# Attention scores of a 16-head transformer stack: from 96-row stacks of four heads to 32x128 row tiles, one strip of partitions per head

## The reference

```python
scores = einsum('bqhd,bkhd->bhqk', q, k) * scale      # per head, contraction over 8
scores = where(mask == 0, -1e9, scores)               # in A2, AS, A3 only
attn   = softmax(scores, axis=-1)
out    = einsum('bhqk,bkhd->bqhd', attn, v)
x      = x + out @ wo + bo
```

## Time and profile before

| | |
|---|---|
| runs | 2376.47, 2366.19, 2374.96 us; median 2374.96 |
| span of the profiled execution, first to last instruction | 2364.8 us |
| what lies around it, if it is one of the three runs (the profile does not say which) | 1.4 to 11.7 us |
| TensorE matmuls | 2118.7 us busy, 14264 instructions |
| TensorE weight loads | 1391.1 us, beside the matmuls |
| VectorE | 1247.3 us |
| ScalarE | 1289.5 us |
| GpSimd | 499.4 us |
| mean granted TensorE clock | 0.932 of 2.4 GHz |
| HBM traffic | 117.53 MB, 49 GB/s over the span |

### The profile page before, as it was taken

How to read it: one execution, slowest core, us unless ns; L and a number is a source line. 1 busy time by engine, 2 the same in 40 slices (tenths; PEclk the granted TensorE clock), 3 DMA queues, 4 the chain that set the end, 5 groups by cost and what they waited for, 6 DMA issues and landing times. The chain is left out here.

```text
span 2364.8 us, 46942 instructions
## 1 busy us (share of the span) xinstructions
PE 2118.7 (90%) x14264; PEld 1391.1 (59%) x14264; DVE 1247.3 (53%) x3806; ACT 1289.5 (55%) x2226; POOL 499.4 (21%) x1107
## 2 busy tenths in 40 slices
PE   2999975699997999979999978887997999989998
PEld 1555543355555889844554545555885555548887
DVE  5667646566662222256666544444564667642343
ACT  0777752377774444346666644444331787864443
POOL 4221210111211222121111111222232222212221
PEclk9999987699998999979999978788997899999999
DMA  3322310622310000052213011110003423300000
GB/s 81 90 80 54 94 29 0 169 71 64 89 40 10 1 0 0 1 143 67 69 45 85 28 41 42 54 54 10 0 0 101 119 72 76 89 1 1 4 4 10
DMA packets 101314, 117.53 MB, mean 50 GB/s; under 512 B 12710, under 2 KB 68412, under 8 KB 101180
## 3 DMA queue, kind: packets, MB, share of 16 engines
q1 hardware_dynamic: 101180, 115.94, 18.5%
HBM read 70.82 MB, written 45.09 MB: 49 GB/s over the span
## 5 line engine op out<-in xcount | busy, mean ns | idle before, releaser
L929 PE MATMUL ps_s<-kst,qz 96*128 96x512 f32 (+2 forms) x1280 | 601.2, 485 | 60.6 <-DMA qz<-q_parts 40.4
L758 ACT ACTIVATE prob<-ps_t 128x512 f32<-128x512 f32 (+1 forms) x896 | 492.3, 581 | 265.7 <-PE ps_t L941 109.9
L941 PE MATMUL ps_t<-qz,kst 128*128 128x512 f32 (+1 forms) x1152 | 464.5, 407 | 0.5 <-ACT prob L758 0.2
L1313 DVE CUSTOM_DVE_ANT_0 junk<-ps_s,mask_q 128x512 bf16<-128x512 f32 x512 | 342.1, 688 | 167.1 <-PE ps_s L929 160.4
L1304 DVE TENSOR_REDUCE mx<-ps_s 128x1 f32<-128x512 f32 x512 | 334.5, 684 | 138.5 <-PE ps_s L929 137.3
L929 PEld LDWEIGHTS ps_s<-kst,qz 96*128 96x128 f32 x1280 | 256.4, 205 | 237.1 <-DVE mx L1313 59.9
L961 PE MATMUL ps_av<-prob,vaug 128*32 128x256 f32 (+1 forms) x4608 | 363.5, 390 | 3.4 <-ACT avs L794 3.1
L1160 PEld LDWEIGHTS ps_s<-w_ffn,prob 128*128 128x128 f32 x2688 | 315.4, 192 | 8.7
L1160 PE MATMUL ps_s<-w_ffn,prob 128*128 128x128 f32 x2688 | 319.2, 276 | 0.0
L798 ACT ACTIVATE qz<-ps_m 32x1024 fp32r<-32x1024 bf16 x160 | 162.7, 1017 | 152.6 <-PE ps_m L971 149.0
L941 PEld LDWEIGHTS ps_t<-qz,kst 128*128 128x128 f32 x1152 | 225.0, 197 | 33.7 <-issue 9.8
(11 more groups left out here) (200 smaller groups left out, 2403.3 us busy)
## 6 DMA issues: line engine op xcount, KB each, us to landing
kst<-k_parts SPq DMA_DIRECT2D x32, 768.0 KB, 6.1
k_parts<-k_hi SPq DMA_DIRECT2D x64, 256.0 KB, 2.9
qz<-q_parts SPq DMA_DIRECT2D x160, 96.0 KB
q_parts<-q_hi SPq DMA_DIRECT2D x80, 128.0 KB, 2.4
ctxT<-in_ctxT SPq DMA_DIRECT2D x32, 256.0 KB, 4.7
k_parts<-k_lo SPq DMA_DIRECT2D x32, 256.0 KB, 2.9
q_parts<-q_lo SPq DMA_DIRECT2D x40, 128.0 KB, 2.4
w_ffn<-in_F_w SPq DMA_DIRECT2D x18, 256.0 KB, 3.9
```

What stands on the lines that cost most here:

```text
L758: nc.scalar.activation(dst, src, ACT.Exp, bias=bias).then_inc(sig["exp_done"], 1)
L929: pe.matmul(ps_s[TURN[i]][:, 0:nk], qz[p][0:96, g, j, q * 128:(q + 1) * 128], kst[p][0:96, g, 0:nk], start=True, stop=True).then_inc(sig[" ...
L941: mm = pe.matmul(dst, kst[p][:, g, kt * 128:(kt + 1) * 128], qz[p][:, g, 2 * half:2 * half + 2, q0:], start=True, stop=mask in (None, "keys"))
L1313: dve.tensor_tensor_reduce(junk[:, TURN[i], 0:nk], src, m, 1.0, -3.0e38, ALU.add, ALU.max, mx[:, buf, i:i + 1])\
```

## The change

The head gets a strip of 32 partitions (24 rows of parts, 8 of the maxima or of ones), and each score matmul contracts over its strip of 32 rows only, as a 32x128 tile of the array. `HEAD_S` and `HEAD_T` say which head's strip a beat uses: the transposed scores of beat n use strip (n+2) mod 4, the scores for the maxima strip n mod 4.

- `qz` with its zeros goes; `qst` holds 32 rows a head, `kst` likewise. The maxima are added in `maxima_T`: one fp32r identity matmul brings `qst` into PSUM and two bf16 matmuls add the three pieces, and ScalarE copies 256 columns into `qmx`, from which `scores_T` reads.
- `scores_T` takes one head and two key tiles: two matmuls of 256 columns on one strip with two weight loads where there was one of 512 columns for two heads. The mask of A2 and of AS is still one identity matmul of 128 rows behind them. In A3 the key mask becomes a matmul of one row (a row of the strip) behind each score matmul: one behind `scores`, two in `scores_T`.
- With the mask in PSUM, VectorE's maxima in A3 are plain reductions, and ScalarE's exponentials have no bias. All maxima are taken negated, so GpSimd's multiplication by -1 goes.
- `k_hi` and `q_hi` are written by GpSimd from `kf` and `qf`, except in AS.
- SyncE loads each group by itself: two DMAs for each of four groups, where there were one for the keys and four for the queries. The semaphores are per group.
- In a beat the transposed scores are issued first, the scores for the maxima second. In AS the four units of transposed scores stand at k = 0 and k = 3 (before: k = 0 and k = 2).
- Setup: `qz` and `kst` are not filled any more; `q_lo`, `k_lo`, `ident_r`, `ones_b` are, and four DMAs write the fill rows to the scratch.

The core of the diff:

```diff
+HEAD_S = [0, 1, 2, 3, 0, 1, 2, 3]
+HEAD_T = [2, 3, 0, 1, 2, 3, 0, 1]
...
+            def load_strips(ph, bt):
+                p, nk = bt.parity, ATT[ph]["nk"]
+                sp.wait_ge(k_saved[p], saved(ph, bt))
+                sp.wait_ge(q_saved[p], saved(ph, bt))
+                for g in range(NG):
+                    sp.dma_start(kst[p][:, g, 0:nk].bitcast(F32), scratch["k"][p][128 * g:128 * (g + 1), 0:nk]).then_inc(stacked[p][g], 16)
+                    sp.dma_start(qst[p][:, g, :].bitcast(F32), scratch["q"][p][128 * g:128 * (g + 1), :]).then_inc(stacked[p][g], 16)
...
             def split_k(ph, bt):
                 pool.wait_ge(sig["k_read"], cnt.at("k_read", ph, bt))
+                if ph != "AS":
+                    apart(pool)
+                    pool.tensor_copy(k_hi[:, 0:nk], kf[:, 0:nk]).then_inc(sig["k_hi_done"], 1)
+                pool.wait_ge(sig["k_hi_done"], cnt.at("k_hi_done", ph, bt))
...
             def maxima_T(ph, bt, g):          # ScalarE
-                nc.scalar.activation(qz[bt.parity][96:128, g, :, :], ps_mb[96:128, :].rearrange("p (j s) -> p j s", j=HG),
-                                     ACT.Copy).then_inc(sig["mt_read"], 1)
+                nc.scalar.activation(qmx[:, g % 2, :], ps_m[:, 0:S], ACT.Copy).then_inc(sig["mt_read"], 1)
...
             def scores(ph, bt, g, i):         # TensorE
-                p, nk, j, q = bt.parity, ATT[ph]["nk"], i // 2, i % 2
+                p, nk, j, q = bt.parity, ATT[ph]["nk"], HEAD_S[i], i // HG
+                strip = slice(STRIP * j, STRIP * (j + 1))
-                pe.matmul(ps_s[TURN[i]][:, 0:nk], qz[p][0:96, g, j, q * 128:(q + 1) * 128], kst[p][0:96, g, 0:nk],
-                          start=True, stop=True).then_inc(sig["s_ready"], 1)
+                mm = pe.matmul(dst, qst[p][strip, g, q * 128:(q + 1) * 128], kst[p][strip, g, 0:nk],
+                               start=True, stop=ATT[ph]["mask"] != "keys")
+                if ATT[ph]["mask"] == "keys":
+                    mm = pe.matmul(dst, ones_b[STRIP * j:STRIP * j + 1, 0:128], mrow[STRIP * j:STRIP * j + 1, p, :], start=False, stop=True)
...
             def scores_T(ph, bt, g, n):
-                mm = pe.matmul(dst, kst[p][:, g, kt * 128:(kt + 1) * 128], qz[p][:, g, 2 * half:2 * half + 2, q0:],
-                               start=True, stop=mask in (None, "keys"))
+                for c in range(2):
+                    kt = 2 * kp + c
+                    dst = bank[:, S * c:S * (c + 1) - seen(ph, kt)]
+                    mm = pe.matmul(dst, kst[p][strip, g, kt * 128:(kt + 1) * 128], qmx[strip, g % 2, seen(ph, kt):],
+                                   start=c == 0 or mask in (None, "keys"), stop=mask is None)
+                    if mask == "keys":
+                        mm = pe.matmul(dst, mrow[STRIP * j:STRIP * j + 1, p, kt * 128:(kt + 1) * 128], ones_b[STRIP * j:STRIP * j + 1, :],
+                                       start=False, stop=True)
                 if mask == "full":
+                    mm = pe.matmul(bank[:, :].rearrange("p (c s) -> p c s", c=2), ident_b[:, :], mask_T[:, 2 * kp:2 * kp + 2, :],
+                                   start=False, stop=True)
...
             def maxima_T(ph, bt, g):          # TensorE
-                for j in range(HG):
-                    for q in range(QT):
-                        mm = pe.transpose(ps_mb[96:128, S * j + 128 * q:S * j + 128 * (q + 1)],
-                                          mpart[:, g % 2, q, 32 * j:32 * j + 32], ident_b[:, :])
+                pe.matmul(ps_m[:, 0:S], ident_r[:, :], qst[bt.parity][:, g, :], start=True, stop=False)
+                for q in range(QT):
+                    mm = pe.matmul(ps_m[:, 128 * q:128 * (q + 1)], mpart[:, g % 2, q, :], ident_b[:, :], start=False, stop=q == QT - 1)
...
                             for half in range(2):
+                                if unit_at(ph, k, half) is not None:
+                                    scores_T(ph, bt, g, unit_at(ph, k, half))
                                 if ahead[0]:
                                     scores(*ahead, 2 * k + half)
-                                if kt is not None:
-                                    scores_T(ph, bt, g, kt, half)
```

More of the change, by code:

```diff
@@ L361, in seen, with pairs, unit, unit_at @@
             return 128 * kt if ph == "AS" else 0
-        def turn_of(ph, g, kt, half):
-            return (2 * (ATT[ph]["nk"] // 128 * g + kt) + half) % 8
+        def pairs(ph):
+            return ATT[ph]["nk"] // (2 * 128)
+        def unit(ph, g, n):
+            return HG * pairs(ph) * g + n
+        def unit_at(ph, k, half):
+            if pairs(ph) == 2:
+                return 2 * k + half
+            return {0: 0, 3: 2}[k] + half if k in (0, 3) else None
+        def chance(ph, g, n):
+            return prob[:, g % 2, HEAD_T[n], :], 2 * (n // HG)
         def slots(ph):
@@ L426, in _ @@
             load_attention("A0", loaded_first)
+            sp.wait_ge(setup_pool, 3)
+            for p in range(2):
+                for n, fill, w in (("q", q_lo, S), ("k", k_lo, SK)):
+                    rest = scratch[n][p].rearrange("(h b c) w -> b h c w", h=H, b=STRIP // DH)[PARTS]
+                    sp.dma_start(rest, fill[:, 0:w].bitcast(F32)).then_inc(strips_filled, 16)
             def load_rest():
@@ L748, in _, with exponentials @@
         def _(act):
-            def exponentials(ph, bt, g, kt, half):
-                p, nkt, q0 = bt.parity, ATT[ph]["nk"] // 128, seen(ph, kt)
-                bias = mcol[:, p, kt:kt + 1] if ATT[ph]["mask"] == "keys" else 0.0
-                wait(act, "st_ready", cnt.at("st_ready", ph, bt, 2 * (nkt * g + kt) + half))
-                if half == 0:
-                    wait(act, "av_ready", cnt.at("av_ready", ph, bt, nkt * g + kt) - 2 * nkt)
-                dst = prob[:, g % 2, kt, 2 * S * half:2 * S * (half + 1)].rearrange("p (j s) -> p j s", j=2)[:, :, q0:]
-                src = ps_t[TURN[turn_of(ph, g, kt, half)]][:, 0:2 * (S - q0)].rearrange("p (j s) -> p j s", j=2)
-                nc.scalar.activation(dst, src, ACT.Exp, bias=bias).then_inc(sig["exp_done"], 1)
+            def exponentials(ph, bt, g, n):
+                nkt = ATT[ph]["nk"] // 128
+                wait(act, "st_ready", cnt.at("st_ready", ph, bt, unit(ph, g, n)))
+                if n % HG == 0:
+                    wait(act, "av_ready", cnt.at("av_ready", ph, bt, nkt * g + 2 * (n // HG) + 1) - 2 * nkt)
+                row, kt = chance(ph, g, n)
+                w = 384 if ph == "AS" else 2 * S
+                nc.scalar.activation(row[:, S * kt:S * kt + w], ps_t[TURN[unit(ph, g, n) % 8]][:, 0:w], ACT.Exp).then_inc(sig["exp_done"], 1)
             def misc(what, ph, bt):
@@ L957, in values @@
                         wait(pe, "v_read", cnt.at("v_read", ph, bt))
-                wait(pe, "exp_done", cnt.at("exp_done", ph, bt, 2 * (nkt * g + kt) + 1))
+                wait(pe, "exp_done", cnt.at("exp_done", ph, bt, unit(ph, g, HG * (kt // 2) + HG - 1)))
                 buf = g % 2
```

171 lines of the change are left out of this document (81 added, 90 removed).

## The result

The changed kernel takes 2636.03 us (median of 4 runs, 2604.12 to 2693.75), the kernel before 2372.03 (median of 4). The ratio, 1.099 with a 95% interval of 1.093 to 1.105, is that of the two faster runs of the changed kernel, 2604.12 and 2617.57 us at mean granted clocks of 0.782 and 0.777, where the slowest had 0.748. Slower, as forecast, but by 264 us by the medians instead of 107, and outside the range of 2335 to 2580. The profiled run is that of 2654.48 us.

The account below looks back on a forecast made before the run. TensorE's order of work was taken to bound four phases. A1 -33, A0 -27, A2 +65, A3 +78, AS +27 and phase starts -3 gave +107 on 2364.8; with 10.2 to the median, 2482 us, range 2335 to 2580.

Parts of the forecast that it names:

- the clock being what it is: Condition on AS's term of +27 us (bounds 0 and +60): the granted clock was taken as unchanged.
- rival (d): TensorE's work looks thinner and the clock falls, mean 0.9 in the four dense phases: 2620 us, chance 0.05.
- I assume that matmuls start in order: TensorE's pairs: in-order starts, different strips overlapping, give pairs of 1.28 us in A1 and 2.24 in A3.
- rival (a): Strips run free of each other, a free strip's matmul starting past a waiting one; A3's pair 1.27: 2340 us, chance 0.11.
- Slower: Sign for the whole kernel: 2482 us, +107 us from the summed terms; slower given 0.73.
- The price of a change of kind: TensorE between 32-row and 128-row matmuls: 0.13 us into the mask, 0.20 out of it.
- (b): Changes of kind between 32-row and 128-row work cost nothing: 2323 us, chance 0.09.
- A2's +65: A2: pair 2.59 us against 2.17 from the mask's changes of kind, plus slots, +8.1 us a batch, +65 us.
- Strips overlap: TensorE's score matmuls on different strips were assumed to overlap, taking an A0 or A1 pair from 1.72 to 1.28 us.
- (c): Strips don't overlap, A0 and A1 pairs stay 1.72 us: 2662 us, chance 0.07.
- VectorE as next limit: A0 and A1: maxima take 1.21 us a pair, so VectorE limits next; 0.7 us a batch given back.
- Costed at nothing: ScalarE's saved copies, GpSimd's `k_hi` and `q_hi`, SyncE's loads (hidden, some 4 us to spare) and setup: no cost within phases.

Follow-up runs that it names:

- e12: Changed kernel with both beats of a pair putting transposed scores and scores for the maxima on the same strip instead of different ones: 3037.94 us (one run).
- e7: Changed kernel with the maxima of A0 and A1 taken over 256 of the 512 scores: 2560.61 us (one run).
- e10: Changed kernel with a 128-row matmul of 512 columns ahead of each score for the maxima in A0 and A1: 3287.4 us (one run).
- e11: e1's order with two 128-row matmuls of 512 columns added together per pair in A0 and A1, AS filled as in e9: 2304.75 us (median of 4).
- e1: Changed kernel, TensorE reordered: each pair issues both transposed scores, both scores, then both masks together, then the values: 2259.79 us (median of 4).
- e6: Changed kernel with each score matmul for the maxima issued three times in A0 and A1, on its strip: 2823.64 us (one run).
- e8: e1's kernel with each score matmul for the maxima issued four times in AS: 2313.15 us, ratio to the kernel before 0.971.
- e9: e1's kernel with two zero-adding 128-row matmuls of 256 columns ahead of each causal mask in AS: 2243.51 us (median of 4).
- e5: Changed kernel with a 128-row bf16 matmul of 512 columns, then overwritten, ahead of each score for the maxima in A2: 2634.7 us (one run).

## Why the prediction was wrong, step by step

- **The clock, which the sum left as it was, is the step that made the miss.** The five phases were summed at the clock of the kernel before ("the clock being what it is"), and a fall of the clock, rival (d), was given 0.05. It fell to 0.59 in A2 and 0.50 in AS and cost some 400 us more than before, by the estimate above; (d) had spread a mean of 0.9 over four phases, 138 us. Its reason, TensorE's work looking thinner, isn't borne out as it stands: TensorE is busy 578 of A2's 606 us.
- **"I assume that matmuls start in order"** is the other step that failed, and its error has the other sign. It made A3's pair 2.24 and A1's 1.28; where nothing outside TensorE holds them up they are 1.27 and 1.02. 1.27 is the very lower bound I had worked out, and rival (a)'s figure. Rival (a)'s mechanism is true and its time is not. The Trainium skill ("TensorE: Matmul & The Clock Gate", The mechanism, in Part 3: starts and ends strictly in program order) decided me; the trace doesn't agree for starts on different row strips (A3's L955 and L974 above; e12). What spoke against (a) in the old timeline were matmuls over the same rows, which can't show it.
- **"Slower" came true by luck.** It was forecast from order and changes of kind, +107 us. By the estimate above the phases' work is some 95 us shorter at full clock, A3 by 23 where I had +78, AS by 20 where I had +27, A0 and A1 by 52 and 55 where I had 27 and 33; only A2 is longer. The clock turned the sign.
- **The price of a change of kind** was right: A2's pair is 2.49 at full clock, forecast 2.59, so (b) is out. Into the mask it is 0.10 (0.43 from T's start, less 0.11 for its load and 0.22 for its two halves), where I took 0.13. Out of it it is 0.11 to empty (steps of 0.32 less 0.215) and 0.11 for the next weight load, which lies behind a matmul's recorded start, as in the earlier trace rows: 0.22, where I took 0.20. A2's +65, slots included, is +57 by the estimate above; the clock added the other 195.
- **Strips overlap**: (c) is out.
- **VectorE as next limit** was right in kind (e7), yet no phase forecast came out: A0 270 and A1 260 (each 250), A2 606 (395), A3 314 (355), AS 326 (285).
- **Costed at nothing**: the new loads are hidden within the phases. TensorE waited for a stack only at phase starts, 4.9 to 5.2 us in A1, A2 and A3 instead of 8.1 to 8.5; in AS, where it had waited six times for `kst` (0.8 to 2.0 us each), not at all. The second context came later, with waits of 9.17, 4.51 and 4.84 us in these three, where the longest was 2.45. The setup, which I had at nothing, is 10 us shorter (first score at 39.4 us instead of 49.0).

What lowers the clock, as far as it is shown: interleaving 128-row matmuls singly among 32-row ones (e10 against e11, the changed kernel's A2 against e1), and 32-row work with few strips side by side (e6, e8, e12). What raises it: 128-row work in a block (e9, e11), and less waiting between 32-row matmuls on four strips (e7). Why these go together was not measured; TensorE's busy share isn't the reason, since e10's A1 has 100% at 0.55. How much a strip counts is open, and so is A3's half-clock time, from 56 to 193 us in six traces of the same code, which nothing here took apart. Filler operands were the identity with zeros, in e5 with the mask; what other data would do was not tried. The Trainium skill (the same page, Part 1, What's actually happening) says that activity releases the throttle; the trace agrees in direction only (e7), since TensorE can be busy throughout and be at half clock (e10).

## What to carry to other kernels

Small row tiles on different strips truly overlap here, but mixed with full-row matmuls one by one they cost a change of kind each and then the clock: group each kind, and keep all four strips full. Price a change of tile shape at both clock levels before summing, since a phase that enters at half clock can stay there (A2's pair 4.25 us instead of 2.49). Judge TensorE by the granted clock beside its busy share; 100% busy went with 0.55 here (e10).

## Not expected of the hardware

The clock's state lasts. e10's A0 and A1 and the changed kernel's A2 begin at half clock and don't leave it for long. Windows of A2 in the changed kernel, ahead of its first rise, in it, and behind it:

```profile
957.00:1104.00 147.00, 135.79 (x469) 60.12 (x475) 50.59 (x149) 42.01 (x75) 13.00 (x40) 0.50 0.23 72
1104.20:1158.60 54.40, 52.88 (x327) 26.23 (x332) 29.51 (x93) 26.49 (x49) 8.72 (x26) 1.00 0.19 57
1158.80:1401.00 242.20, 234.70 (x853) 103.34 (x870) 78.22 (x253) 69.78 (x128) 22.66 (x62) 0.50 0.12 38
```

The same loop ran for 54 us at 1.00 and then for 242 at 0.50, and TensorE busy 97% of both. What TensorE did before it rose is visible: the slot V is eight 128-row matmuls in a row, 2.08 us at half clock, and the rises at 1104.1 and 1401.1 come at the ends of two such blocks, here the first:

```profile
1102.14 2.08 PE L1034 MATMUL ps_m<-w_A,ctxT 128*128 128x128 f32 x8
1104.14 0.50 PE L971 MATMUL ps_t<-qmx,kst 32*128 32x256 f32 x2
```

In the four traces with A2's code unchanged all 8 rises between its pairs lie within 0.5 us of the end of such a block, and 11 more blocks met at half clock raised nothing. Which of them raise it differs from run to run, and with it A2's 329 to 565 us of half. That is a reading of the traces; no run moved these blocks.

And work that does nothing made a phase faster: AS took 250 us in e1's trace and 222 and 224 in those of e9 and e11.
